# Flamingo gated block on one core: chunk 14's second half earlier inside chunk 15, a new order of the prologue and of chunks 0 and 1

## The reference

```
# step 1, a recurrence over the 128 positions, all 32 batch entries at once
q = layernorm(x)
r      = decay * r + ctx_t * ctx_t
inp    = (q_t * r) @ Wi.T + bi
gate   = sigmoid(inp @ Wg.T + bg)
state  = tanh((gate*state + (1-gate)*inp) @ A.T + inp @ Bm.T)
x1     = x + tanh(g_xattn) * (state @ Wo.T + bo)
# step 2, a feed-forward layer with ternary weights, 256 -> 1024 -> 256
Wq = clip(round(W / (mean|W| + 1e-5)), -1, 1)
out = x1 + tanh(g_ffn) * (relu(layernorm(x1) @ Wq1.T + b1) @ Wq2.T + b2)
```

## Time and profile before

| what | value |
|---|---|
| three runs | 318.69, 318.70, 319.15 us; median 318.7 us |
| the profiled execution's own time | 318.8 us |
| its span, first to last instruction | 316.9 us |
| mean granted TensorE clock | 0.994 of full speed |
| PE matmul busy | 302.3 us (95%), 3784 instructions |
| DVE busy | 280.9 us (89%), 810 |
| ACT busy | 238.5 us (75%), 560 |
| POOL (GpSimd) busy | 81.9 us (26%), 142 |

### The profile page before, as it was taken

One profiled execution on the slowest core, in us unless ns is written; L12 is line 12 of the kernel. 1 busy time (PEld: TensorE's weight loads), 2 busy tenths in 40 slices (PEclk: granted clock), 3 DMA queues, 4 the chain that ended last, 5 costly groups with the idle time before them and its releaser, 6 DMA issues. The chain is left out here.

```text
span 316.9 us, 10128 instructions
## 1 busy us (share of the span) xinstructions
PE 302.3 (95%) x3784; PEld 276.4 (87%) x3784; DVE 280.9 (89%) x810; ACT 238.5 (75%) x560; POOL 81.9 (26%) x142
## 2 busy tenths in 40 slices
PE   7988689999999999999999999999999999999995
PEld 5767578899999999999999999999999999997784
DVE  5887699999999999999999999999999998968763
ACT  4677658787777787877877777878777777757693
POOL 3321133241321413141413213131414121141230
PEclk9999979999999999999999999999999999999999
DMA  7931415113343434251424434441514214171321
GB/s 257 395 97 52 100 35 97 55 33 54 135 68 134 68 126 76 83 108 39 127 40 132 66 132 66 131 67 63 126 36 132 41 66 66 69 101 37 66 35 66
DMA packets 19543, 29.16 MB, mean 92 GB/s; under 512 B 1856, under 2 KB 10304, under 8 KB 19392
## 3 DMA queue, kind: packets, MB, share of 16 engines
q0 software_dynamic: 8720, 8.39, 18.6%
q1 hardware_dynamic: 10368, 19.93, 17.9%
q10 hardware_dynamic: 432, 0.53, 0.5%
HBM read 16.26 MB, written 4.19 MB: 65 GB/s over the span
## 5 line engine op out<-in xcount | busy, mean ns | idle before, releaser
L481 ACT ACTIVATE state<-pre_ps,sc 128x64 f32<-128x64 f32 x128 | 39.9, 312 | 48.7 <-PE pre_ps L1082 47.4
L471 ACT ACTIVATE hid<-hid_ps,b_s 128x256 f32<-128x256 f32 x120 | 50.2, 470 | 11.0 <-PE hid_ps L1121 9.3
L1121 PE MATMUL hid_ps<-xt_lo,w_q 128*128 128x256 f16 x240 | 55.5, 272 | 0.0
L1133 PE MATMUL y_ps<-w_q,h_lo 128*128 128x256 bf16 x240 | 55.5, 272 | 0.0
L1133 PE MATMUL y_ps<-w_q,h_hi 128*128 128x256 bf16 x240 | 55.5, 272 | 0.0
L1121 PE MATMUL hid_ps<-xt_hi,w_q 128*128 128x256 f16 x240 | 55.5, 272 | 0.0
L1076 PE MATMUL pre_ps<-m_hi,a_hi 128*128 128x32 f16 x508 | 42.6, 178 | 4.7 <-DVE m_hi L701 4.5
L752 DVE TENSOR_TENSOR h_lo<-hid,h_hi 128x512 f16<-128x512 f32 x60 | 41.3, 688 | 3.1 <-ACT h_hi L477 1.4
L1076 PEld LDWEIGHTS pre_ps<-m_hi,a_hi 128*128 128x128 f16 x508 | 33.8, 96 | 10.6 <-DVE m_hi L701 6.5
L1076 PE MATMUL pre_ps<-m_hi,a_lo 128*128 128x32 f16 x508 | 41.5, 176 | 0.0
L477 ACT CAST h_hi<-hid 128x512 f16<-128x512 f32 x60 | 37.1, 619 | 1.9
(11 more groups left out here) (181 smaller groups left out, 895.7 us busy)
## 6 DMA issues: line engine op xcount, KB each, us to landing
x_norm<-x_in SPq DMA_DIRECT2D x16, 256.0 KB, 2.7
cx<-ctx_in SPq DMA_DIRECT2D x16, 256.0 KB, 3.0
x_res<-x_in SPq DMA_DIRECT2D x16, 256.0 KB, 3.2
x_res<-bo_g POOLq DMA_DIRECT2D x16, 256.0 KB, 4.8
x<-b_g POOLq DMA_DIRECT2D x15, 256.0 KB, 3.8
y_out<-y SPq DMA_DIRECT2D x15, 256.0 KB, 2.0
w_raw<-w_in SPq DMA_DIRECT2D x2, 512.0 KB, 7.3
w_raw<-w_in SPq DMA_DIRECT2D x1, 1024.0 KB, 9.4
```

The lines of the kernel that those rows point to most:

```text
L471: last = nc.scalar.activation(hid[:, p % 2, u, :], hid_ps[p % 2][:, u * N:(u + 1) * N], ACT.Relu, bias=b1_s[:, 2 * p + u:2 * p + u + 1], s ...
L481: nc.scalar.activation(state[:, q[1] % 2, :, step_cols(j)], pre_ps[q[1] % 2][:, :].rearrange("p (k n) -> p k n", k=K)[:, :, step_cols(j)], ...
L1121: last = nc.tensor.matmul(hid_ps[p % 2][:, u * N:(u + 1) * N], w1_q[:, k, cut], v[:, par, k, :], start=n == 0, stop=n == len(terms) - 1)
L1133: last = nc.tensor.matmul(y_ps[:, t * D:(t + 1) * D], h[:, f, t * P:(t + 1) * P], w2_q[:, f, :], start=f == 0 and t == 0 and h is h_hi, st ...
```

## The change

It moves work and adds none, but for two more `keep_warm` matmuls in chunk 0.

- Prologue: the first statistics of chunk 1's layernorm are cut in two, one half ahead of mx_t and one behind mx_d. Five of the scales (one-column operations) go from DVE to POOL. The products b2_g and bo_g of rows and gates go from the end of chunk 0 to behind `square((0, 1))` on ACT, and the DMA of rows is issued two DMAs earlier on SP.
- Chunk 0: `half_sum(3)` stands ahead of tanh 5; the gate product's high terms ahead of step 5 and its low terms behind it; `wo_lo` and gpart go up by one or two steps; the two `side_sign` at steps 6 and 7 leave chunk 0.
- Chunk 1: the scan at step 0 stands ahead of `state_low`. Signs and ternaries are spread anew over chunks 1 and 2.
- Chunk 15 alone: on DVE `finish(12)` and `residual(14)` go from step 2 to 1, the statistics and h_lo 1 from 3 to 2, `x1_apply` from 5 to 3, h_lo 2 from 4 to 3, `normed_low` from 7 to 5. On ACT `normed_high` goes from 6 to 5. On PE both halves of the output product stand at step 0 and `x1_t` at 4; `hidden_product(14, 0)` comes into step 6 and `hidden_product(14, 1)` with `end_output(0)` into step 7.
- The end: PE, DVE and ACT without what moved; on PE y_product 0 and 1 of chunk 14 now stand ahead of `end_transpose(0)`.

The diff, with unchanged lines cut and the indentation of inner lines reduced:

```diff
...
-        SIGN_AT = {(0, 6): 0, (0, 7): 2, (1, 0): 1, (1, 2): 3, (1, 4): 4, (1, 6): 5, (1, 7): 6, (2, 1): 7}
-        TERNARY_AT = {(1, 0): 0, (1, 1): 2, (1, 3): 1, (1, 5): 3, (2, 0): 4, (2, 1): 5, (2, 3): 6, (2, 4): 7}
+        SIGN_AT = {(1, 0): 0, (1, 1): 2, (1, 2): 1, (1, 4): 3, (1, 6): 4, (1, 7): 5, (2, 1): 6, (2, 3): 7}
+        TERNARY_AT = {(1, 1): 0, (1, 3): 2, (1, 5): 1, (1, 7): 3, (2, 0): 4, (2, 1): 5, (2, 3): 6, (2, 5): 7}
         CHUNK, NEXT_CHUNK, THIRD = (0, 0), (0, 1), (0, 2)
...
         QUARTERS = 4
-        PREP = ["zero", "keep", "mx", "mx_t", "mx_d", "bound", "top", "inv", "s_ch", "bm_lo", "aw_lo", "s_a", "sc",
+        PREP = ["zero", "keep", "mx", "mx_t", "mx_d", "bound", "top", "inv", "s_ch", "bm_lo", "aw_lo",
         "a_lo", "wo_lo", "gpart", "gmean", "thr", "gates_out"]
...
         done = {name: n + 1 for n, name in enumerate(PREP)}
-        APREP = ["gates", "wi", "wg", "bm", "aw", "a", "wo", "sums", "bo_b2"]
-        PPREP = ["wi_lo", "wg_lo"]
+        APREP = ["gates", "wi", "wg", "bm", "aw", "a", "bo_b2", "wo", "sums"]
+        PPREP = ["wi_lo", "wg_lo", "s_a", "sc"]
         pdone = {name: n + 1 for n, name in enumerate(PPREP)}
...
     load_norm((0, 1))
+    sp.dma_start(rows[:, :, :], rows_in).then_inc(rows_in_s, 16)
     sp.dma_start(w1_raw[:, 1, :], w1_in[:, 1, :]).then_inc(w1_in_s[1], 16)
     sp.dma_start(w2_raw[:, :, :], w2_in).then_inc(w2_in_s, 16)
-    sp.dma_start(rows[:, :, :], rows_in).then_inc(rows_in_s, 16)
...
     whole_low("wg", wg_hi, wg_lo, WG)
+    pool.wait_ge(dve_prep, done["inv"])
+    nc.gpsimd.tensor_scalar(S_A, inv[:, 0:1], WEIGHT_TOP, None, ALU.mult).then_inc(pool_prep, 1)
+    nc.gpsimd.tensor_scalar(I_CH, pow2[:, 0:1], 1.0 / (WEIGHT_TOP * STATE_SCALE), None, ALU.mult)
+    nc.gpsimd.tensor_scalar(S_WO, inv[:, 1:2], WEIGHT_TOP, None, ALU.mult)
+    nc.gpsimd.tensor_scalar(S_X, inv[:, 2:3], HIDDEN_TOP / HIDDEN_SCALE, None, ALU.mult)
+    nc.gpsimd.tensor_scalar(S_H, inv[:, 2:3], HIDDEN_TOP, None, ALU.mult).then_inc(pool_prep, 1)
     rstd1_of(NEXT_CHUNK)
...
     gate_out((0, 0))
-    act.wait_ge(dve_prep, done["s_a"])
+    act.wait_ge(pool_prep, pdone["s_a"])
     scaled_high(a_hi, WA, S_A)
...
     square((0, 1))
+    act.wait_ge(act_prep, adone["gates"])
+    act.wait_ge(rows_in_s, 16)
+    nc.scalar.mul(b2_g[:, :], rows[:, 1, :], gates[:, 1:2])
+    nc.scalar.mul(bo_g[:, :], rows[:, 0, :], gates[:, 0:1]).then_inc(act_prep, 1)
...
     def first():
+        act.wait_ge(pool_prep, pdone["sc"])
         tanh_step(CHUNK, 0)
...
         ret_high(NEXT_CHUNK)
-        act.wait_ge(dve_prep, done["sc"])
         scaled_high(wo_hi, WO, S_WO)
...
         tanh_step(CHUNK, 4)
+        half_sum(3).then_inc(act_prep, 1)
         tanh_step(CHUNK, 5)
-        half_sum(3).then_inc(act_prep, 1)
         gate_out(NEXT_CHUNK)
...
         square(THIRD)
-        act.wait_ge(act_prep, adone["gates"])
-        act.wait_ge(rows_in_s, 16)
-        nc.scalar.mul(b2_g[:, :], rows[:, 1, :], gates[:, 1:2])
-        nc.scalar.mul(bo_g[:, :], rows[:, 0, :], gates[:, 0:1]).then_inc(act_prep, 1)
-        side_sign(0)
-        side_sign(2)
...
                     square(norm)
-            if j == 6:
-                if project:
-                    rest_high(project)
-                if attend:
-                    normed_high(attend)
-                if norm:
-                    norm_apply(norm)
+            if j == 6 and project:
+                rest_high(project)
+            if attend and j == (5 if peeled == NC - 1 else 6):
+                normed_high(attend)
+            if j == 6 and norm:
+                norm_apply(norm)
+            if j == 7 and peeled == NC - 1:
+                hidden(NEXT, 0)
...
     end_state_high(1)
-    for p in (0, 1):
-        hidden(NEXT, p)
-        hidden_high(NEXT, p)
+    hidden_high(NEXT, 0)
+    hidden(NEXT, 1)
+    hidden_high(NEXT, 1)
     end_normed_high(0)
...
     prep("mx", nc.vector.tensor_reduce(mx[:, 1:2], wsq[WO][:, :, :], AX.XY, ALU.max, apply_absolute_value=True))
+    dve.wait_ge(x_norm_in[1], landed(NEXT_CHUNK))
+    nc.vector.bn_stats(st1[:, 0, :], x_norm[:, 1, 0, :])
     dve.wait_ge(pe_prep, 1)
...
     prep("mx_d", nc.vector.tensor_scalar(mx_d[:, :], ident[0:3, 0:3], mx_t[:, :], None, ALU.mult))
-    norm_stats(NEXT_CHUNK)
+    nc.vector.bn_stats(st1[:, 1, :], x_norm[:, 1, 1, :]).then_inc(stats1, 1)
     dve.wait_ge(pe_prep, 2)
...
     inp_low((0, 0))
+    dve.wait_ge(stats1, upto(NEXT_CHUNK))
     norm_mean(NEXT_CHUNK)
...
     scaled_low("aw", aw_hi, aw_lo, WA, S_CH)
-    prep("s_a", nc.vector.tensor_scalar(S_A, inv[:, 0:1], WEIGHT_TOP, None, ALU.mult))
-    nc.vector.tensor_scalar(I_CH, pow2[:, 0:1], 1.0 / (WEIGHT_TOP * STATE_SCALE), None, ALU.mult)
-    nc.vector.tensor_scalar(S_WO, inv[:, 1:2], WEIGHT_TOP, None, ALU.mult)
-    nc.vector.tensor_scalar(S_X, inv[:, 2:3], HIDDEN_TOP / HIDDEN_SCALE, None, ALU.mult)
-    prep("sc", nc.vector.tensor_scalar(S_H, inv[:, 2:3], HIDDEN_TOP, None, ALU.mult))
     rest_all((0, 0))
...
         norm_mean(THIRD)
+        scaled_low("wo", wo_hi, wo_lo, WO, S_WO)
         gated_state(CHUNK, 5)
         inp_low(NEXT_CHUNK)
+        sums_of_partition()
         gated_state(CHUNK, 6)
-        scaled_low("wo", wo_hi, wo_lo, WO, S_WO)
-        sums_of_partition()
         norm_apply(THIRD)
...
         rest_low(NEXT_CHUNK)
+        dve.wait_ge(pool_prep, pdone["sc"])
         gates_of_columns()
...
         peeled = c[1] if isinstance(c[0], int) else None
+        last = peeled == NC - 1
         for j in range(T):
...
                     norm_stats(norm)
+                if peeled == 1:
+                    scan(project)
                 if attend:
...
                     norm_mean(norm)
-                if peeled == 1:
-                    scan(project)
             if j == 1:
...
                     ret_low(project)
-                if exists(plus(c, -3)):
-                    finish(plus(c, -3))
-                if attend:
-                    residual(attend)
-                if peeled == 1:
-                    norm_stats(norm)
-                    norm_mean(norm)
-            if j == 3:
-                if attend:
-                    x1_stats(attend)
-                if ffn:
-                    hidden_low(ffn, 1)
-                if attend:
-                    x1_mean(attend)
+            if exists(plus(c, -3)) and j == (1 if last else 2):
+                finish(plus(c, -3))
+            if attend and j == (1 if last else 2):
+                residual(attend)
+            if j == 2 and peeled == 1:
+                norm_stats(norm)
+                norm_mean(norm)
+            if attend and j == (2 if last else 3):
+                x1_stats(attend)
+            if ffn and j == (2 if last else 3):
+                hidden_low(ffn, 1)
+            if attend and j == (2 if last else 3):
+                x1_mean(attend)
             if j == 4:
...
                     inp_low(project)
-                if ffn:
+                if ffn and not last:
                     hidden_low(ffn, 2)
-            if j == 5:
-                if attend:
-                    x1_apply(attend)
-                if ffn:
-                    hidden_low(ffn, 3)
+            if attend and j == (3 if last else 5):
+                x1_apply(attend)
+            if ffn and last and j == 3:
+                hidden_low(ffn, 2)
+            if j == 5 and ffn:
+                hidden_low(ffn, 3)
             if j == 6:
...
                     scan(norm)
-            if j == 7:
-                if project:
-                    rest_low(project)
-                if attend:
-                    normed_low(attend)
-                if ffn and peeled == NC - 1:
-                    finish(ffn)
+            if j == 7 and project:
+                rest_low(project)
+            if attend and j == (5 if last else 7):
+                normed_low(attend)
+            if last and j == 7:
+                finish(ffn)
             if peeled == NC - 1:
...
         step(CHUNK, 4)
-        keep_warm(8)
+        keep_warm(10)
+        pe.wait_ge(inp_hi_set, upto(NEXT_CHUNK))
+        high_terms(ret_ps, wg_hi, wg_lo, inp_hi)
         step(CHUNK, 5)
-        gate_product(NEXT_CHUNK)
-        step(CHUNK, 6)
+        pe.wait_ge(inp_lo_set, upto(NEXT_CHUNK))
+        low_terms(ret_ps, wg_hi, inp_lo).then_inc(gate_sum, 1)
         pe.wait_ge(dve_prep, done["gpart"])
         nc.tensor.matmul(y_ps[:, 0:2], ones[:, :], gpart[:, :], start=True, stop=True).then_inc(pe_prep, 1)
+        step(CHUNK, 6)
         from_inp(NEXT_CHUNK, 0)
...
                 normed_t(project)
-            if j < TILES and attend:
+            if attend and (j == 0 if peeled == NC - 1 else j < TILES):
                 if peeled == 1 and j == 0:
                     pe.wait_ge(dve_prep, done["wo_lo"])
-                output_product(attend, j)
+                for t in range(TILES) if peeled == NC - 1 else (j,):
+                    output_product(attend, t)
```

(14 more changed lines are left out.)

## The result

The changed kernel took **320.96 us** (median of 20 runs, 319.28 to 322.44), the kernel before, run beside it, 319.16 (20 runs, 318.69 to 322.10). The medians are 1.8 us apart. The ratio over all runs is 1.0042, 95% interval 1.0022 to 1.0062, which is 1.3 us; it is less because five of the runs before took 320.17 to 322.10. Forecast were 319.1 and a range from 317.6 to 320.4.

The account below looks back on a forecast made before the run. PE bounds the middle, ACT and DVE order chunks 0 and 1, the DVE-ACT recurrence chunk 15. From 318.8 us, 3.85 early and 4.2 late gave 319.15, with the median 0.1 lower 319.1; range 317.6 to 320.4.

Parts of the forecast that it names:

- the fourth rival: Chunk 15: PE's clock falls to half in its new holes, costing up to 1.7 us, time 320.8; chance 0.08.
- part 1: Prologue and chunks 0 to 2: the new order is 3.85 us early in sum, bounds 3.1 to 4.5.
- m_hi(15,6): Chunk 15, DVE: 3.15 us late, since xt_lo and s_lo now stand ahead of it.
- tanh(15,7): Chunk 15, ACT: 3.35 us late, with PE doing y 6 and 7 and hidden_product(14,0) ahead of step 7.
- part 2: Chunk 15 and the end: the new order is 4.2 us late in sum, bounds 3.1 to 4.6.
- the ternary at (1,7): Chunk 1, step 7, DVE: one more ternary ahead of m_hi(2,0) adds 0.65 us that nothing gives back.
- signs and ternaries together: Chunks 1 and 2: their new places gain about 1.1 us at m_hi(1,1), less 0.65 at (1,7): 0.45.
- The half clock near 40 us is no gain of its own: Chunk 1: the half clock goes as PE's hole shrinks from 2.2 to 1.1 us; no gain, DVE was late anyhow.
- Five scales on POOL: Prologue: takes 0.5 us of DVE's scales from ahead of rest; on POOL they take 1 to 3.2 us, no loss counted.
- No half clock near 40 us: Chunk 1: sign that the forecast is right, PE's stretch at the 1.2 GHz level is gone after the change.
- The end swallows part: The end takes in part of chunk 15's delay, leaving 2.6 us late and a time of 317.5; chance 0.15 together.
- DVE gives back the start: DVE from (1,7) to (2,2) has no idle, so the early start shrinks to 2.7 us, time 320.2; chance 0.15.

Follow-up runs that it names:

- e3: The changed kernel plus 12 and 14 unread matmuls in PE's two longest holes, at chunk 15's steps 1 and 5: 319.52 us, ratio 1.0009.
- e2: The changed kernel with the old prologue and chunks 0 to 2, keeping the new chunk 15 and end: 324.59 us, ratio 1.0155.
- e11: Against e1, the old maps of signs and ternaries, with two signs at the end of chunk 0: 316.37 us, ratio 0.9896.
- e10: Against e1, all five scales back on DVE ahead of rest: 315.63 us, ratio 0.9867.
- e9: The changed kernel with 14 unread matmuls behind chunk 15's step 5 only, step 1's hole left open: 320.56 us, ratio 1.0017.
- e1: The changed kernel with the old chunk 15 and end, keeping the new prologue and chunks 0 to 2: 314.96 us, ratio 0.9872.
- e4: Against e1, ternaries 1 and 3 at (1,4) and (1,5) instead of (1,5) and (1,7): 314.63 us, ratio 0.9847.
- e6: Against e4, chunk 15's xt_hi at step 5 and xt_lo at step 6, behind m_hi(15,6): 314.10 us, ratio 0.9837.

## Why the prediction was wrong

The step that failed is the clock in chunk 15: the sum has no term for it, and the fourth rival, "the clock falls in chunk 15", was given 0.08. It is the usual case: 19 of 20 runs lost clock somewhere, and the profiled one there. The missing term measures 1.6 us in the profiles (e3) and 1.3 to 1.5 in the medians (320.8 in the middle group, 319.3 to 319.5 at full clock). The rival's price was put at up to 1.7 and the time at 320.8; the runs of the middle group have 320.01 to 321.26. The price was right, the chance was not. The argument against it, that between the new holes PE works while before it was at 0.00 for over 2 us, read one row as a bound: the row showed a hole that was enough, and said nothing of what smaller one would be. The range cut off just below the time that the same text had worked out for this rival.

Point by point, with 0.27 taken off the starts up to chunk 15, and 3.57 the head start there:

| step | forecast | in the profile |
|---|---|---|
| tanh(0,0) | 0.8 early | 20.02 - 19.54 + 0.27 = 0.75 |
| gate(1) | 1.25 early | 29.90 - 29.07 + 0.27 = 1.10 |
| m_hi(1,1) | 4.45 early | 39.05 - 34.98 + 0.27 = 4.34 |
| part 1, at h_lo(13,0) | 3.85 early | 285.80 - 282.23 + 0.27 = 3.84 |
| m_hi(15,3) | 1.5 late | 286.43 - 288.46 + 3.57 = 1.54 |
| m_hi(15,4) | 1.9 late | 288.90 - 290.53 + 3.57 = 1.94 |
| m_hi(15,6) | 3.15 late | 293.69 - 294.15 + 3.57 = 3.11 |
| tanh(15,7) | 3.35 late | 298.07 - 296.95 + 3.57 = 4.69 |
| first `end_hidden_product` | 4.0 late | 305.02 - 302.87 + 3.57 = 5.72 |
| last DVE operation | 4.2 late | 316.50 - 314.20 + 3.57 = 5.87 |

Down to m_hi(15,6) nothing is off by over 0.15. Then 1.3 us appear at once, between 293.69 and 298.07, where the windows show the half clock, and stay to the end, where they have become 5.87 - 4.2 = 1.67, the 1.6 of e3's comparison. e3, without the stretch, gives 319.5, and part 2 is 4.2 in e2's one run at the clock of before and 4.3 in e3's profile. So **the sums of part 1 and part 2 were right, the clock was missing.** Inside part 1 the ternary at (1,7) was put too high, which the sum hid, and signs and ternaries together came out too low for it (1.1 - 0.35 is near the 0.7 that e11 shows). The largest share, 2.7, was seen only at the points of the table and has no run of its own.

- *"The half clock near 40 us is no gain of its own"* held for the stretch that the prediction read: the kernel before at clock 0.999, one run, took 318.96, no less than at 0.993. The stretch of 6.8 us in e2's profile cost 1.0. In the new order one costs 1.0 to 1.5 (e10's profiled run, e9's tanh(1,5), e1's 316.43 against 315.0); that this is because DVE is no longer late there is argued, not shown. "No half clock near 40 us" held in the profile, not in every run.
- *Five scales on POOL.* Their sum is 13.72 to 16.48 = 2.8 us, within the 1 to 3.2. Nothing was lost: DVE's inp_lo beside them took 0.69. The Trainium skill ("SBUF — State Buffer", "Who interferes with whom") has a two-input DVE operation and a reading GpSimd one contend. The trace agrees on POOL's side: the three that start inside one of DVE's two-input operations end 0.06 to 0.07 behind it (14.60 behind inp_lo's 14.53, 15.42 behind bm_lo's 15.35, 16.20 behind aw_lo's 16.14), and the two that start just ahead of one take 0.24 and 0.21. It shows no DVE operation as the loser.
- *Ternary at (1,7)*: a term of 0.65 that e4 measures at 0.35 by the medians, 0.57 by the profiles.
- *The other rivals.* "The end swallows part" falls: the end took nothing back (e2). "DVE gives back the start" falls: at h_lo(13,0) the start was all there.

The Trainium skill ("TensorE: Matmul & The Clock Gate", "HAM oscillation — how this bites in real kernels") says that waits between bursts of matmuls drop the clock again and that it is paid each time. The trace agrees, at 294.9 us, behind a wait of 1.65. The prediction had it as a rival by name and went by the one, longer hole that it had seen. That it is paid each time is more than these runs show: the same wait had no fall behind it in e2.

## What to carry to other kernels

Work hung ahead of a recurrence's next operation on a strict queue was paid in full here (m_hi 1.5 us late from step 1, 0.4 more from step 3, 1.2 more from step 5): walk that queue with the trace's durations, and put the moved work behind the operation (e6) rather than ahead of it. When a move opens holes on PE like those here (1.47 and 1.65 us of waiting), price the half clock that may follow, ask whether PE is late there, and give it a large chance: here 19 of 20 runs fell with both holes open, 7 of 12 with one filled, 2 of 12 with both. Where times of one kernel fall into groups, sort the runs by granted clock before comparing medians; here that alone shows a 319.3 kernel inside a 321.0 one.

## What the runs showed of the hardware

- A wait of 1.65 us of PE was followed, 0.9 us after its end, by 3.4 us at the 1.2 GHz level. It cost 1.6 there, where PE is needed. In chunk 1 before, where DVE is late, 3.4 us of it cost nothing (one run without it) and 6.8 us cost 1.0 (e2).
- Behind the same hole the clock falls or doesn't from one execution to the next: 41 to 42 us with PE at 0.24 and no fall in the changed kernel, at 0.20 and a fall in e9; in the same chunk 15, a fall behind step 5's wait of 1.65 in the changed kernel, behind step 1's of 1.47 and not behind step 5's in e2.
- Twelve and fourteen unread matmuls of 128x256 in the holes (1.69 us for the 14) raised the share of runs without a fall from 1 of 20 to 10 of 12; the fourteen alone, on another chip, to 5 of 12.
- POOL's one-column operations range from 0.21 to 0.76 us for the same work. Those that start inside a two-input operation of DVE last until 0.06 to 0.07 us behind its end; DVE's own durations stay (inp_lo 0.69).
